# Up is kept in HBM in place of a second computation, and quantised values are rounded by 16-bit results

## The chip, the cores and the metric

The kernel runs on one core of one Trainium2 chip. The metric is the time of one execution on the device in microseconds, lower is better. The engines meant here are TensorE (PE in the profile), VectorE (DVE), ScalarE (ACT), GpSimd (POOL) and SyncE (SP), which issues transfers.

## The reference

Two decoder layers over x of 32 x 128 x 256 (batch, sequence, feature) in float32, with a context of the same shape. Each layer is a cross attention and a feed-forward part, each behind a layer norm and added to x. The change touches only the last feed-forward part, in which every tensor is quantised by its own largest absolute value:

```python
def act_qdq(x):                      # 16 bits, one scale for the whole tensor
    scale = jnp.maximum(jnp.max(jnp.abs(x)) / 32767.0, 1e-12)
    return jnp.clip(jnp.round(x / scale), -32768.0, 32767.0) * scale
def fixed_qdq_u16(x):
    return jnp.clip(jnp.round(x * 65536.0), 0.0, 65535.0) / 65536.0
x = act_qdq(layernorm(x))
up = act_qdq(x @ dequant(w_up).T)            # 4096 x 768
gate = act_qdq(x @ dequant(w_gate).T)        # 4096 x 768
sig = fixed_qdq_u16(sigmoid(gate))
gate = act_qdq(gate * sig)
o = act_qdq(gate * up)
return o @ dequant(w_down).T                 # added to x
```

Each scale needs the peak of a whole tensor of 4096 x 768 values, so nothing can be rounded before the last value of the tensor exists.

## The kernel before

The 4096 tokens lie along the free dimension, the 768 hidden features in six groups of 128 partitions (IC = 6). Work goes by "quads" of 512 tokens (NQ = 8) or by "pieces" of 256 tokens (2 x NQ = 16; 128 x 1536 elements). The whole Gate tensor stays in SBUF in float32 (`wide`, 96 KB of each partition). The quantised input stays as int16 (`xqT`) and GpSimd widens it quad by quad to float32 (`widen`, line 577, tile `xqs`, two buffers). There is no room for a second tensor like `wide`, so Up is computed twice: once for its peak alone, once for its values.

Each engine has its own hand-written program, and semaphores tie them together. In order:

- Gate (to about 849 us). `hidden` (line 1144) multiplies; ScalarE copies to `wide` (762); VectorE takes the peak (1562). `make_unit(n, count)` (1521 to 1541) turns a peak into a scale: reduce to one column, TensorE transposes it (`spread_peak(n)`, 1121) so that all partitions see all values, and eight small VectorE operations follow. Unit 1 is Gate's, 2 Up's, 3 that of Gate times sigmoid, 4 the product's, and spread_peak(n) serves unit n.
- Stage one, 16 pieces. TensorE computes Up a first time (1144, pass k = 1) and VectorE reads its peak from PSUM (1587), which frees the bank. ScalarE rounds Gate by adding the magic number 1.5 x 2^23 (777) and subtracting it (782), takes the sigmoid (788), multiplies by 65536 and adds the magic number (792). VectorE subtracts it (1592), multiplies sigmoid and Gate (1597) and takes the peak (1601). In this stage unit 2 is made after the last piece, and unit 3 right behind it. TensorE's program has spread_peak(3) behind the first quad of its next pass.
- Stage two, 8 quads. TensorE computes Up again (pass k = 2), ScalarE rounds it out of PSUM (802) and rounds the gated values (809), VectorE subtracts the magic number (1611), multiplies (1617) and takes the peak (1621).
- The tail, 32 sequences: ScalarE rounds (817), VectorE subtracts (1631), TensorE multiplies by Down (1175), VectorE adds to x (1636), SyncE stores.

The lines that set the order on TensorE between the stages:

```python
for k, freed, last_freed in ((1, up_peak, hid_kept), (2, up_round, up_peak)):
    pe.wait_ge(last_freed, NQ * IC)
    if k == 2:
        spread_peak(2)
    for t in range(2):
        hidden(t, t, wuT, k * NQ, freed)
        if k == 2 and t == 0:
            spread_peak(3)
```

Of the kernel before, what the change touches and what calls it, by code (L numbers as in the profile page):

```python
# [20 lines left out]
I16 = mybir.dt.int16  # L21
U32 = mybir.dt.uint32
# [6 lines left out]
DC = D // 128  # L29
# [18 lines left out]
LN_PARTS = (slice(0, 28), slice(28, B))  # L48
MAGIC = 1.5 * 2.0 ** 23
# [147 lines left out]
def build(nc, x, ctx_in, wq, wk, wv, wo, bq, bk, bv, bo, wfr, wfi, bf, wval, bval, woff, boff,  # L197
# [3 lines left out]
    outr = out.rearrange("b l d -> l b d")  # L201
    with ExitStack() as ctx:
# [3 lines left out]
        def sb(name, shape, dt=F32, scope=ctx):  # L206
# [20 lines left out]
        unit = sb("unit", [128, 8, 8])  # L227
        wgT = sb("wgT", [128, DC, I])
# [7 lines left out]
        wide = sb("wide", [128, IC, B * L], F32, ffn)  # L236
        xqT = sb("xqT", [128, DC, B * L], I16, ffn)
        xqs = sb("xqs", [128, 2, DC, QUAD * L], F32, ffn)
        sig_place = ExitStack()
        sig = sb("sig", [128, 2, IC, 256], F32, sig_place)  # L240
        sig_place.close()
        up_place = ExitStack()
        ups = sb("ups", [128, 2, IC, QUAD * L], F32, up_place)
        up_place.close()
# [191 lines left out]
        def _(sp):  # L436
# [7 lines left out]
            sp.dma_start(sel_f[:], c_sel).then_inc(load_sel, 16)  # L444
            sp.wait_ge(x3_done, 2 * NQ)
# [6 lines left out]
        def _(pool):  # L452
# [131 lines left out]
            with pool.Fori(0, NQ // 2) as i:  # L584
                for u in range(2):
                    widen(i * 2 + u, u, NQ)
            for t in range(2):
                widen(t, t, 2 * NQ)
            with pool.Fori(1, NQ // 2) as i:
                for u in range(2):  # L590
                    widen(i * 2 + u, u, 2 * NQ)

        @block.scalar
        def _(act):
# [180 lines left out]
            def round_gate(t, s):  # L775
                g = wide[:, :, at_piece(t)]
                nc.scalar.activation(g, g, ACT.Identity, scale=unit[:, 1, 3:4], bias=unit[:, 7, 0:1]).then_inc(g_round, 1)  # L777

            def whole_gate(t, s):
                act.wait_ge(g_round, t + 1)  # L780
                g = wide[:, :, at_piece(t)]
                nc.scalar.activation(g, g, ACT.Copy, bias=-MAGIC).then_inc(g_whole, 1)

            def sigmoid(t, s):
                act.wait_ge(g_whole, t + 1)
                if late(t, 2):
                    act.wait_ge(g2_done, t - 1)
                nc.scalar.activation(sig[:, s], wide[:, :, at_piece(t)], ACT.Sigmoid, scale=unit[:, 1, 2:3]).then_inc(sig_done, 1)

            def round_sigmoid(t, s):  # L790
                act.wait_ge(sig_done, t + 1)
                nc.scalar.activation(sig[:, s], sig[:, s], ACT.Copy, scale=65536.0, bias=MAGIC).then_inc(sig_round, 1)

            act.wait_ge(unit_step, 1 + 2 * 5)
            staggered(act, 2 * NQ, [(0, round_gate), (2, whole_gate), (5, round_sigmoid), (4, sigmoid)])

            def round_up(t, s):
                if late(t, 2):
                    act.wait_ge(o_done, t - 1)
                for oc in range(IC):  # L800
# [22 lines left out]
        def _(pe):  # L823
# [334 lines left out]
            for k, freed, last_freed in ((1, up_peak, hid_kept), (2, up_round, up_peak)):  # L1158
                pe.wait_ge(last_freed, NQ * IC)
                if k == 2:  # L1160
                    spread_peak(2)
# [498 lines left out]
```

## Time and profile before

| | |
|---|---|
| median of 3 runs | 1166.85 us (1166.5 to 1167.36) |
| the profiled execution | 1167.25 us |
| its span, first to last instruction | 1165.3 us |
| mean granted TensorE clock | 0.94 |
| busy: PE, DVE, ACT, POOL | 966.7, 739.4, 506.2, 279.5 us |
| HBM read, written | 15.22 MB, 4.19 MB |

A busy share is an average over stages that have different limits. The rows below therefore go by stage, in microseconds from the start of the span. "128x1536 f32" is a tile of 128 partitions by 1536 elements. Where two instructions of one engine follow each other closely, their busy times overlap by about 0.1 us, so the distance between their starts is the better price. One float32 matmul of the source is two records. "Idle before" is the engine's idle time ahead of an instruction, with what ended it.

### The profile page before, as it was taken

Reading aid. Unit: us, or ns where it says so; the run is one execution under the profiler, and the core shown is the slowest. Engines: PE = TensorE matmul, PEld = TensorE weight load, DVE = VectorE, ACT = ScalarE, POOL = GpSimd, SP = SyncE. Lnnn points to the kernel's source line nnn. Section 1 sums busy time; section 2 is a strip of 40 time slices with the busy share of each in tenths; the row PEclk is TensorE's granted clock in tenths of the full one; section 3 lists DMA queues with packets and bytes.
Section 4 is the critical chain, followed back from the end, with each engine's and each line's share of the span. In section 5 each row is a group of like instructions: output and inputs, shape, how many; then the busy total and the mean of one; then the engine's idle time right before and its main releaser. Section 6 shows DMA issues by size and latency. Waiting matters only on the chain.

```text
span 1165.3 us, 15427 instructions
## 1 busy us (share of the span) xinstructions
PE 966.7 (83%) x4829; PEld 599.1 (51%) x4829; DVE 739.4 (63%) x1246; ACT 506.2 (43%) x853; POOL 279.5 (24%) x251
## 2 busy tenths in 40 slices
PE   1399998899797977758888888699968975994998
PEld 1377776688465755424444444344423332441887
DVE  4377777555473566547888888744428995787333
ACT  0132221311122434346666666134369962764332
POOL 0300000132103111047877887200100010100000
PEclk9999999999898988859999999799998996997999
DMA  9500000000000000000000000000000000000111
GB/s 320 194 1 0 0 0 0 1 0 0 10 0 0 1 1 0 0 1 1 1 1 1 1 2 1 1 0 1 0 1 0 0 0 0 1 0 0 36 54 54
DMA packets 18216, 19.97 MB, mean 17 GB/s; under 512 B 1201, under 2 KB 17531, under 8 KB 18046
## 3 DMA queue, kind: packets, MB, share of 16 engines
q1 hardware_dynamic: 12950, 12.86, 3.4%
q10 hardware_dynamic: 5224, 6.57, 1.7%
q8 instruction: 24, 0.39, 0.1%
q14 instruction: 18, 0.15, 0.0%
HBM read 15.22 MB, written 4.19 MB: 17 GB/s over the span
## 4 chain that ended last, share of the span: by engine, by line
PE 38%; DVE 8%; POOL 6%; ACT 5%; issue 4%; DVEq 0%; ACTq 0%
PE pair L1144 16%; PE pair L1175 7%; POOL hat L552 4%; PE pair L1064 3%; PE pair L1078 3%; DVE peak L1587 1%; PE pair L1040 1%; PE pair L1048 1%; ACT down_b L736 1%; DVE wide L1597 1%; ACT wide L777 1%; DVE hat L1464 1%; PE pair L1090 1%; PE pair L1010 1%; PE pair L1130 1%
## 5 line engine op out<-in xcount | busy, mean ns | idle before, releaser
L1144 PE MATMUL pair<-xqs,wuT 128*128 128x512 f32 x384 | 173.9, 611 | 18.7 <-DVE peak L1587 18.0
L552 POOL TENSOR_TENSOR hat<-hat 128x1024 f32<-128x1024 f32 x62 | 145.8, 2363 | 45.6 <-DVE hat L1464 44.9
L1144 PEld LDWEIGHTS pair<-xqs,wuT 128*128 128x128 f32 x384 | 73.8, 196 | 117.4 <-issue 83.8
L1048 PE MATMUL pair<-rows,sel 32*128 32x512 bf16 x256 | 75.4, 397 | 22.9 <-ACT down_b L736 17.3
L1464 DVE SCALAR_TENSOR_TENSOR hat<-pair,down_a 128x1024 f32<-128x1024 f32 x64 | 78.2, 1222 | 24.2 <-PE pair L1040 19.7
L577 POOL CAST xqs<-xqT 128x1024 f32 (+1 forms) x24 | 25.0, 1041 | 271.0 <-PE pair L1144 192.9
L1175 PE MATMUL pair<-wdT,hid 128*128 128x256 f32 x384 | 85.5, 387 | 3.0 <-DVE hid L1631 3.0
L1464 DVE SCALAR_TENSOR_TENSOR hat<-pair,down_b 128x1024 f32<-128x1024 f32 x64 | 78.2, 1221 | 11.9 <-PE pair L1040 11.7
L736 ACT ACTIVATE down_b<-pair 128x512 f32<-128x512 f32 x128 | 69.4, 596 | 37.1 <-PE pair L1048 32.2
L1144 PE MATMUL pair<-xqs,wgT 128*128 128x512 f32 x192 | 85.2, 601 | 0.0
L736 ACT ACTIVATE down_a<-pair 128x512 f32<-128x512 f32 x128 | 69.5, 595 | 33.3 <-PE pair L1048 23.7
L1175 PEld LDWEIGHTS pair<-wdT,hid 128*128 128x128 f32 x384 | 74.6, 194 | 13.8 <-DVE hid L1631 3.2
L1064 PE MATMUL pair<-hat,vz 128*32 128x128 f32 x1056 | 69.9, 278 | 2.8 <-POOL hat L552 2.5
L1064 PEld LDWEIGHTS pair<-hat,vz 128*32 128x32 f32 x1056 | 52.9, 110 | 25.1 <-issue 24.3
L861 PE MATMUL pair<-wT,ft_sb 128*128 128x256 f32 x256 | 63.8, 392 | 0.0
L1187 DVE BATCH_NORM_STATS2 stats<-x_sb 128x6 f32<-128x256 f32 (+1 forms) x128 | 49.8, 417 | 16.5 <-DMA x_sb<-in_x_dram 16.5
L1340 DVE TENSOR_TENSOR x_sb<-pair,x_sb 128x256 f32 (+1 forms) x64 | 27.2, 424 | 51.6 <-PE pair L935 33.5
L1144 PEld LDWEIGHTS pair<-xqs,wgT 128*128 128x128 f32 x192 | 36.6, 194 | 43.6 <-issue 43.5
L817 ACT ACTIVATE hid<-wide,unit 128x768 f32 (+1 forms) x32 | 32.5, 1025 | 58.2 <-DVE hid L1631 46.1
L802 ACT ACTIVATE ups<-pair,unit 128x512 f32<-128x512 f32 x48 | 36.3, 774 | 40.1 <-PE pair L1144 40.0
L762 ACT ACTIVATE wide<-pair 128x512 f32<-128x512 f32 (+1 forms) x48 | 28.7, 597 | 56.9 <-PE pair L1144 56.9
L634 ACT ACTIVATE q_sb<-pair 128x256 f32<-128x256 f32 x32 | 12.3, 383 | 93.3 <-PE pair L865 93.3
(207 smaller groups left out, 1862.5 us busy)
## 6 DMA issues: line engine op xcount, KB each, us to landing
x_sb<-in_x_dram SPq DMA_DIRECT2D x8, 512.0 KB, 12.2
c_sb<-in_ctx_dram SPq DMA_DIRECT2D x8, 512.0 KB, 16.6
out_dram<-x_sb SPq DMA_DIRECT2D x16, 256.0 KB, 2.1
four<-in_c_four_dram ACTq DMA_DIRECT2D x1, 1280.0 KB, 12.2
deq<-in_L_ffn_w_gate_dram ACTq DMA_DIRECT2D x1, 768.0 KB, 12.7
deq<-in_L_ffn_w_up_dram ACTq DMA_DIRECT2D x1, 768.0 KB, 16.0
deq<-in_L_ffn_w_down_dram ACTq DMA_DIRECT2D x1, 768.0 KB, 16.5
big<-in_c_big_dram ACTq DMA_DIRECT2D x1, 448.0 KB
```

Source lines behind the costliest of these rows:

```text
L552: nc.gpsimd.tensor_tensor(hat[:, n % RING, :], hat[:, (n - 2) % RING, :], hat[:, n % RING, :], ALU.add).then_inc(summed, 1)
L736: nc.scalar.activation(down[n % 2][:, i, :], bank[6 + i], ACT.Relu).then_inc(down_done, 1)
L802: nc.scalar.activation(ups[:, s, oc, :], bank[2 + oc][:], ACT.Identity, scale=unit[:, 2, 3:4], bias=unit[:, 7, 0:1]).then_inc(up_round, 1)
L817: nc.scalar.activation(hid[:, 2 + s], wide[:, :, at_seq(b)], ACT.Identity, scale=unit[:, 4, 3:4], bias=unit[:, 7, 0:1]).then_inc(o_round, 1)
L861: mm(bank[2 + s][:, i * D:(i + 1) * D], ft_sb[:, s, i * DC + c, :], wT[:, i, c, :], start=False, stop=(i == 1 and c == DC - 1))
L1048: mm(bank[6 + i], sel[g:g + 32, pp, 1, :], rows[g:g + 32, q, c * 2 + a, :], start=True, stop=True).then_inc(down_mm, 1)
L1064: last = mm(bank[4 + c][32 * m:32 * m + 32, b * 128:(b + 1) * 128], vz[:, r, b, h:h + 32], hat[:, tile % RING, i * QUAD * L + b * 128:i * ...
L1078: last = mm(bank[5][:, b * D:(b + 1) * D], attT[:, c, (2 * i + b) * L:(2 * i + b + 1) * L], wout_sb[:, c, :], start=False, stop=(b == 1 an ...
L1144: last = mm(bank[2 + oc][:], w[:, c, oc * 128:(oc + 1) * 128], xqs[:, s, c, :], start=(c == 0), stop=(c == DC - 1))
L1175: last = mm(bank[s][:, 0:D], hid[:, s, ic, :], wdT[:, ic, :], start=(ic == 0), stop=(ic == IC - 1))
L1187: V.bn_stats(stats[:, at(b), :].rearrange("p o s -> p (o s)"), x_sb[:, at(b), :].rearrange("p o d -> p (o d)")).then_inc(bn_done, 1)
L1464: V.scalar_tensor_tensor(hat[:, n % RING, :], pair[n % 2][:].rearrange("p i t -> p (i t)"), 0.0, down[n % 2][:].rearrange("p i t -> p (i t ...
```

## The change

Up is computed once. TensorE works in pairs of PSUM banks (two of the six feature groups, 512 tokens; 24 pairs in all). ScalarE copies each pair to an SBUF stage of three buffers, VectorE takes the peak from there, and SyncE stores it to an HBM tensor `up_far`. After TensorE's last pair SyncE loads Up back quad by quad into three slots `ups`, which lie where the int16 input and the first stage's buffers were.

Rounding no longer uses the magic number in these two stages: an operation that multiplies by the scale writes an int16 or uint16 tile, and the conversion rounds and clamps. GpSimd does it for Gate (`whole_gate`), the sigmoid (`whole_sigmoid`) and Up (`whole_up`), ScalarE for the gated values (`whole_g2`). VectorE multiplies 16-bit tiles into float32. Both stages go by 16 halves of 256 tokens, written out instead of looped, and spread_peak(2) and (3) stand behind the last pair on TensorE. Gone are round_gate, whole_gate, round_sigmoid, round_up and round_g2 on ScalarE, the two subtractions whole_sigmoid and whole_up on VectorE, and TensorE's two passes over Up by quads. The fourth unit, the tail and all that comes before Gate are as before.

```diff
+    up_far = nc.dram_tensor("up_far", (128, NQ, IC, QUAD * L), F32, kind="Internal").ap()
+        sq = sb("sq", [128, 2, IC, 256], U16, sq_place)
+        upq = sb("upq", [128, 2, IC, 256], I16, upq_place)
+        ups = sb("ups", [128, 3, IC, QUAD * L], F32, up_place)
+        g2q = sb("g2q", [128, 4, IC, 256], I16, up_place)
-        sig = sb("sig", [128, 2, IC, 256], F32, sig_place)
-        ups = sb("ups", [128, 2, IC, QUAD * L], F32, up_place)
+        gq = sb("gq", [128, 4, IC, 256], I16, gq_place)
+        up_stage = sb("up_stage", [128, 3, 2, QUAD * L], F32, gq_place)
+        def ups_before(h):
+            return range(3 * h // 2, 3 * (h + 1) // 2)
...
@@ sync @@
+            for p in range(UPS):
+                sp.wait_ge(up_kept, p + 1)
+                sp.dma_start(up_far[:, p // 3, 2 * (p % 3):2 * (p % 3) + 2, :], up_stage[:, p % 3]).then_inc(up_stored[p % 3], 16)
+            sp.wait_ge(hid_mm, 2 * NQ * IC)
+            for t in range(NQ):
+                for j in range(3):
+                    sp.wait_ge(up_stored[j], 16 * (t + 1))
+                if t == 2:
+                    sp.wait_ge(g2_done, HALVES)
+                if t >= 3:
+                    sp.wait_ge(up_whole, 2 * (t - 2))
+                sp.dma_start(ups[:, t % 3], up_far[:, t]).then_inc(up_back[t % 3], 16)
...
@@ gpsimd @@
+            def whole_gate(h):
+                if h >= 4:
+                    pool.wait_ge(g2_done, h - 3)
+                nc.gpsimd.tensor_scalar(gq[:, h % 4], gate_half(h), unit[:, 1, 3:4], None, ALU.mult).then_inc(gate_whole, 1)
+            def whole_sigmoid(h):
+                pool.wait_ge(sig_done, h + 1)
+                if h >= 2:
+                    pool.wait_ge(g2_done, h - 1)
+                nc.gpsimd.tensor_scalar(sq[:, h % 2], gate_half(h), 65536.0, None, ALU.mult).then_inc(sig_whole, 1)
+            pool.wait_ge(unit_step, 1 + 2 * 5)
+            whole_gate(0)
+            for h in range(HALVES):
+                if h + 1 < HALVES:
+                    whole_gate(h + 1)
+                whole_sigmoid(h)
+                if h % 2 == 1 and h // 2 + 2 < NQ:
+                    widen(h // 2 + 2, h // 2 % 2, NQ)
+            def whole_up(h):
+                t = h // 2
+                if h % 2 == 0:
+                    pool.wait_ge(up_back[t % 3], 16 * (t // 3 + 1))
+                if h >= 2:
+                    pool.wait_ge(o_done, h - 1)
+                nc.gpsimd.tensor_scalar(upq[:, h % 2], ups[:, t % 3, :, h % 2 * 256:(h % 2 + 1) * 256], unit[:, 2, 3:4], None, ALU.mult).then_inc(up_whole, 1)
+            pool.wait_ge(g2_done, HALVES)
+            pool.wait_ge(unit_step, 1 + 3 * 5)
+            for h in range(HALVES):
+                whole_up(h)
...
@@ scalar @@
+            def keep_up(p):
+                act.wait_ge(hid_mm, NQ * IC + 2 * p + 2)
+                if p >= 3:
+                    act.wait_ge(up_stored[p % 3], 16 * (p // 3))
+                    act.wait_ge(up_peak, p - 2)
+                nc.scalar.activation(up_stage[:, p % 3], pair[1 + p % 3][:], ACT.Copy).then_inc(up_kept, 1)
+            def sigmoid(h):
+                act.wait_ge(gate_whole, h + 1)
+                nc.scalar.activation(gate_half(h), gq[:, h % 4], ACT.Sigmoid, scale=unit[:, 1, 2:3]).then_inc(sig_done, 1)
+            for h in range(HALVES):
+                for p in ups_before(h):
+                    keep_up(p)
+                sigmoid(h)
+            def whole_g2(h):
+                if h >= 4:
+                    act.wait_ge(o_done, h - 3)
+                nc.scalar.activation(g2q[:, h % 4], gate_half(h), ACT.Copy, scale=unit[:, 3, 3:4]).then_inc(g2_whole, 1)
+            act.wait_ge(unit_step, 1 + 4 * 5)
+            for h in range(HALVES):
+                whole_g2(h)
...
@@ tensor @@
+            def up_pair(p):
+                t, j = p // 3, p % 3
+                if j == 0:
+                    pe.wait_ge(xqs_ready, NQ + t + 1)
+                if t:
+                    pe.wait_ge(up_kept, p - 2)
+                else:
+                    pe.wait_ge(hid_kept, (NQ - 1) * IC + 2 * j + 2)
+                for oc in (2 * j, 2 * j + 1):
+                    for c in range(DC):
+                        last = mm(bank[2 + oc], wuT[:, c, oc * 128:(oc + 1) * 128], xqs[:, t % 2, c, :], start=(c == 0), stop=(c == DC - 1))
+                    last.then_inc(hid_mm, 1)
+            for p in range(UPS):
+                if p == 2:
+                    pe.wait_ge(xq_kept, B)
+                    spread_peak(1)
+                up_pair(p)
+            spread_peak(2)
+            spread_peak(3)
...
@@ vector @@
+            def peak_up(p):
+                dve.wait_ge(up_kept, p + 1)
+                V.tensor_reduce(peak[:, 2, p:p + 1], up_stage[:, p % 3], AX.XY, ALU.max, apply_absolute_value=True).then_inc(up_peak, 1)
+            def gated(h):
+                dve.wait_ge(sig_whole, h + 1)
+                V.tensor_tensor(gate_half(h), sq[:, h % 2], gq[:, h % 4], ALU.mult).then_inc(g2_done, 1)
+            for h in range(HALVES):
+                for p in ups_before(h):
+                    peak_up(p)
+                gated(h)
+                if h:
+                    peak_gated(h - 1)
+            dve.wait_ge(up_peak, UPS)
+            make_unit(2, UPS)
+            peak_gated(HALVES - 1)
+            dve.wait_ge(g2_peak, HALVES)
+            make_unit(3, HALVES)
+            def hidden_product(h):
+                dve.wait_ge(up_whole, h + 1)
+                dve.wait_ge(g2_whole, h + 1)
+                V.tensor_tensor(gate_half(h), upq[:, h % 2], g2q[:, h % 4], ALU.mult).then_inc(o_done, 1)
+            for h in range(HALVES):
+                hidden_product(h)
+                if h:
+                    peak_product(h - 1)
+            peak_product(HALVES - 1)
+            make_unit(4, HALVES)
```

## Rows read from the trace of the kernel before

**Rows 1.** Windows by stage: length, busy us (instructions) per engine, clock, DMA share, GB/s.

```profile
856.70:973.40 116.70, 81.94 (x178) 33.51 (x176) 96.51 (x96) 95.45 (x65) 8.33 (x8) 0.88 0.00 0
973.40:989.00 15.60, 15.23 (x31) 6.73 (x32) 3.04 (x16) 4.71 (x7) 1.04 (x1) 0.82 0.00 0
989.00:1073.00 84.00, 70.23 (x164) 30.78 (x162) 68.17 (x24) 53.75 (x50) 5.20 (x5) 0.95 0.00 0
...
1076.70:1165.30 88.60, 85.50 (x384) 74.56 (x384) 30.14 (x63) 30.82 (x31) 0.00 (x0) 0.97 0.14 47
```

**Rows 2.** Chain that ended last, in order of time: start, us, what.

```profile
856.67 4.78 ACT wide L777 x3
...
987.13 72.12 PE pair L1144 x168
```

**Rows 3.** Groups by line and shape from 750 us on: busy us, mean ns.

```profile
L1601 DVE TENSOR_REDUCE peak<-wide x12 | 21.0, 1749 | 0.0
...
L1592 DVE TENSOR_SCALAR sig<-sig 128x1536 f32<-128x1536 f32 x16 | 15.4, 959 | 20.2 <-ACT sig L792 20.0
...
L762 ACT ACTIVATE wide<-pair 128x512 f32<-128x512 f32 x24 | 14.3, 597 | 29.0 <-PE pair L1144 29.0
...
L1621 DVE TENSOR_REDUCE peak<-wide x4 | 13.4, 3346 | 0.0
...
L788 ACT ACTIVATE sig<-wide,unit 128x1536 f32<-128x1536 f32 x8 | 12.6, 1570 | 9.1 <-DVE wide L1597 9.1
...
L755 ACT ACTIVATE xqT<-pair 128x256 int16<-128x256 f32 x14 | 4.9, 383 | 3.2 <-PE pair L1130 2.9
...
L788 ACT ACT_TABLE_LOAD x1 | 1.3, 1283 | 0.0
```

**Rows 4.** VectorE's timeline between the stages: start, us, instruction, idle before.

```profile
968.43 1.76 DVE L1597 SCALAR_TENSOR_TENSOR wide<-sig,wide 128x1536 f32<-128x1536 f32 x1
970.09 3.42 DVE L1601 TENSOR_REDUCE peak<-wide 128x1 f32<-128x1536 f32 x2
...
975.41 0.17 DVE L1521 TENSOR_REDUCE unit<-peak 128x1 f32<-128x16 f32 x1
987.17 0.29 DVE L1523 TENSOR_REDUCE unit<-pair 128x1 f32<-128x128 f32 x1 [11.59 <-PE pair L1121]
...
1073.04 0.16 DVE L1521 TENSOR_REDUCE unit<-peak 128x1 f32<-128x8 f32 x1
```

**Rows 5.** TensorE's timeline, the two transposes and what runs before them.

```profile
849.94 5.42 PE L1144 MATMUL pair<-xqs,wuT 128*128 128x512 f32 x12 [0.69 <-ACT wide L762]
855.19 0.27 PE L1121 MATMUL pair<-big,unit 128*128 128x128 f32 x1
...
974.00 13.02 PE L1144 MATMUL pair<-xqs,wuT 128*128 128x512 f32 x24
```

**Rows 6.** GpSimd's groups over the whole span: busy us, mean ns.

```profile
L552 POOL TENSOR_TENSOR hat<-hat 128x1024 f32<-128x1024 f32 x62 | 145.8, 2363 | 45.6 <-DVE hat L1464 44.9
L577 POOL CAST xqs<-xqT 128x1024 f32 x20 | 20.8, 1041 | 239.1 <-PE pair L1144 171.0 <-ACT xqT L755 68.1
...
L468 POOL COPY cst<-c_sb 128x256 f32 x30 | 12.1, 404 | 131.5 <-PE pair L848 131.5
```

**Rows 7.** VectorE's tensor_scalar groups, and the timeline at 412 us.

```profile
L1401 DVE TENSOR_SCALAR tx<-off 128x512 f32<-128x512 f32 x4 | 7.2, 1804 | 0.0
...
L1407 DVE TENSOR_SCALAR tx<-tx 128x512 f32<-128x512 f32 x4 | 1.7, 416 | 0.0
...
412.22 2.13 POOL L518 TENSOR_TENSOR parts<-ccx,parts 128x1024 bf16<-128x1024 f32 x1 [6.26 <-ACT parts L716]
...
412.39 2.23 DVE L1401 TENSOR_SCALAR tx<-off 128x512 f32<-128x512 f32 x1
```

**Rows 8.** Transfers: a window of the loads, and the page's row of the output stores.

```profile
5.00:25.00 20.00, 3.65 (x16) 3.28 (x16) 9.84 (x28) 0.00 (x0) 0.00 (x0) 1.00 1.09 353
...
out_dram<-x_sb SPq DMA_DIRECT2D x16, 256.0 KB, 2.1
```

More of the change, by code:

```diff
@@ L772, in _ @@
             by_quad(act, keep_quad)
[L775 to L788, printed above, removed]
@@ L790, in round_sigmoid @@
-            def round_sigmoid(t, s):
-                act.wait_ge(sig_done, t + 1)
-                nc.scalar.activation(sig[:, s], sig[:, s], ACT.Copy, scale=65536.0, bias=MAGIC).then_inc(sig_round, 1)
-            act.wait_ge(unit_step, 1 + 2 * 5)
[L795 to L800, printed above, removed]
-                    act.wait_ge(hid_mm, (2 * NQ + t) * IC + oc + 1)
-                    nc.scalar.activation(ups[:, s, oc, :], bank[2 + oc][:], ACT.Identity,
-                                         scale=unit[:, 2, 3:4], bias=unit[:, 7, 0:1]).then_inc(up_round, 1)
@@ L1131, in turn_xq, with hidden @@
                 last.then_inc(xq_turned, 1)
-            def hidden(t, s, w, before, freed):
-                pe.wait_ge(xqs_ready, before + t + 1)
+            def hidden(t, s):
+                pe.wait_ge(xqs_ready, t + 1)
                 for oc in range(IC):
-                    if oc == 3 and isinstance(t, int) and t == 0 and before == NQ:
-                        pe.wait_ge(xq_kept, B)
-                        spread_peak(1)
                     if late(t, 1):
-                        pe.wait_ge(freed, (t - 1) * IC + oc + 1)
+                        pe.wait_ge(hid_kept, (t - 1) * IC + oc + 1)
                     for c in range(DC):
-                        last = mm(bank[2 + oc][:], w[:, c, oc * 128:(oc + 1) * 128], xqs[:, s, c, :], start=(c == 0), stop=(c == DC - 1))
+                        last = mm(bank[2 + oc][:], wgT[:, c, oc * 128:(oc + 1) * 128], xqs[:, s, c, :], start=(c == 0), stop=(c == DC - 1))
                     last.then_inc(hid_mm, 1)
@@ L1150, in gate_quad @@
                         turn_xq((t + 1) * QUAD + k, k % 2)
-                hidden(t, u, wgT, 0, hid_kept)
+                hidden(t, u)
             for k in range(QUAD):
@@ L1155, in _ @@
             by_quad(pe, gate_quad)
[L1158 to L1161, printed above, removed]
-                for t in range(2):
-                    hidden(t, t, wuT, k * NQ, freed)
-                    if k == 2 and t == 0:
-                        spread_peak(3)
-                with pe.Fori(1, NQ // 2) as i:
-                    for u in range(2):
-                        hidden(i * 2 + u, u, wuT, k * NQ, freed)
+            def up_pair(p):
[17 more added lines that the diff above has]
+            spread_peak(3)
             def down_product(b, s):
@@ L1581, in _ @@
             make_unit(1, NQ)
-            def peak_up(t, s):
-                for j in range(IC // 2):
-                    dve.wait_ge(hid_mm, NQ * IC + t * (IC // 2) + j + 1)
-                    V.tensor_reduce(peak[:, 2, at(t * (IC // 2) + j)], bank[2 + s * (IC // 2) + j][:], AX.X, ALU.max,
-                                    apply_absolute_value=True).then_inc(up_peak, 1)
-            def whole_sigmoid(t, s):
-                dve.wait_ge(sig_round, t + 1)
-                V.tensor_scalar(sig[:, s], sig[:, s], MAGIC, 65535.0, ALU.subtract, ALU.min).then_inc(sig_whole, 1)
```

80 lines of the change are left out of this document (29 added, 51 removed).

## The prediction

> **What bounds the kernel now.** I read the page's 40 slices first (TensorE 83% busy, no other engine over 63%), then the chain that ended last, then the windows of the last feed-forward stage by stage, because only there does the diff touch anything. The reader is to see three stages and a tail. In the sigmoid stage (856.7 to 973.4) no engine is idle long: VectorE is busy for 96.5 of 116.7 us and ScalarE for 95.5, TensorE for only 82, and its clock is at 0.88 because it stops and starts [rows 1]. In the product stage (989 to 1073) the chain is TensorE alone, 72.1 us of second Up products in 168 records [rows 2]. Between them lie 15.6 us in which VectorE works for 3 [rows 1]: the transpose that spreads the fourth peak stands behind a tile of 24 Up records that took 13.0 us [rows 5], and VectorE waited 11.6 us for the result [rows 4]. The tail, 88.6 us of Down products, is TensorE's and the change leaves it alone [rows 1].
>
> The sum below is made against the profiled execution, 1167.25 us with a span of 1165.3; the median of the runs is 1166.85, so 0.4 us less.
>
> **Stage one, start.** TensorE runs straight from Gate into Up in pairs of 8 records. A record costs 72.12/168 = 0.43 us [rows 2], a pair 3.43, a half (a pair and a half) 5.15. The second peak's transpose will stand behind two pairs, 6.9 us from 849.3, where Gate ends (849.94 less 0.69 of waiting): at 856.2 instead of 855.19 [rows 5], so 1.0 us later, and the stage starts at 857.7 instead of 856.67 [rows 2]. Then the chain of half 0 has to run: whole_gate on GpSimd (1.5, below), a table load of 1.3 and a sigmoid of 1.6 on ScalarE [rows 3], whole_sigmoid (1.5). VectorE's first product starts at about 863.1 (the table load half hidden).
>
> **Stage one, VectorE.** It loses the subtraction of the magic number (959 ns [rows 3]) and reads Up's peaks in SBUF. Starts of neighbouring 1536-element operations lie 1.66 us apart, product and reduce alike [rows 4]. From 1536 to 3072 elements a reduce grows by 3346 - 1749 = 1597 ns [rows 3], so one of 1024 is 1.66 - 0.53 = 1.13. A half is 1.5 x 1.13 + 1.66 + 1.66 = 5.0 us, against 96.5/16 = 6.0 now. The product of two 16-bit tiles into f32 has no row; I take the f32 one, and as other end the subtraction's 0.96.
>
> **Stage one, ScalarE and TensorE.** Per half ScalarE has 1.5 copies of 128x1024 from PSUM (597 ns for 512 [rows 3], and two fewer fixed parts: at most 1.2, I take 1.03) and one sigmoid of 1.6: 3.2 us where it has 95.5/16 = 6.0 now. An int16 result costs it nothing (383 ns for 256 elements [rows 3]). TensorE needs 5.15, so it and VectorE share the bound at about the same pace. ScalarE's copy of a pair waits for TensorE, for the store and for the peak of three pairs before; the sigmoid stands behind it, and with it GpSimd and VectorE. Three pairs are 10.3 us, so only TensorE's wait can last, and that is the 5.15.
>
> **Stage one, GpSimd.** This is the price that decides. Per half it gets whole_gate and whole_sigmoid (1536 elements, one f32 input, a multiplication, a 16-bit result) and half a widening of 1.04. No row shows such an operation. Lower end: its copies and casts, 404 ns for 256 and 1041 for 1024 elements [rows 6], 0.83 ns an element, so 1.47 us. Upper end: its two-input operation, 2363 ns for 1024 [rows 6], so 3.54. I take 1.5, because one input makes it most like the cast, which also changes between 16-bit and f32: 2 x 1.5 + 0.52 = 3.5 us a half, under the 5.15. The Trainium skill (GPSIMD Engine Reference, Engine selection) says that one-input operations run at roughly line rate there, which gives the same.
>
> **The shared port.** When GpSimd and VectorE overlap, one of them can stand still: VectorE's tensor_scalar of 128x512 takes 416 ns alone and 1804 where a GpSimd operation had begun just before it; the one started at 412.39 ended 0.27 us after GpSimd's 2.13 us operation from 412.22 [rows 7]. New here are GpSimd operations beside VectorE products with two SBUF inputs. Suppose that these exclude each other. GpSimd is released by the end of a product (two sq buffers; upq likewise in stage two) and then works for 3.0 or 4.0 us while VectorE has 2.8 or 3.9 of reduces, which need no second input. That fits almost, so I add only 0.25: a period of 5.25. If every product had to wait for a whole GpSimd operation it would be 6.5. The Trainium skill (SBUF — State Buffer, Who interferes with whom) says as much: a VectorE instruction with two SBUF inputs and a GpSimd one that reads SBUF block each other fully; by it my sum stands only as long as GpSimd stays short.
>
> Stage one: 863.1 + 15 x 5.25 + 1.66 = 943.5 for the last product. Then a reduce 1.66, unit 2, a reduce 1.66, unit 3; a unit without a queue in front is 1.9 to 2.0 us (from the end of the two reduces, 973.5, to 975.41 [rows 4]): 950.8 for unit 3, against 989.0. Of these 38 us, about 26 are the stage and 12 the transpose that no longer stands behind a tile.
>
> **Stage two.** whole_g2 of half 0 adds 1.6: 952.4. TensorE has nothing to do. VectorE has 16 products and 16 reduces of 1.66, 3.32 a half, and 0.08 for waits: 3.4. GpSimd's whole_up (1.5) runs under the reduce (1.66), ScalarE's whole_g2 (1.6) under both. 952.4 + 54.4 = 1006.8 for the reduce of the last peak, which stands at 1073.04 now [rows 4]. Gain 66.2: 1167.25 - 66.2 = 1101.
>
> **The transfers.** Up goes out in 24 stores of 512 KB, one per 3.43 us, and comes back in 8 loads of 1.57 MB. Loads ran at 353 GB/s and a store of 256 KB lands in 2.1 us [rows 8]; in the tail the stores kept the transfer engines 0.14 busy for 47 GB/s [rows 1], so 336 would be their full pace. A store needs 1.6 us of the engines and lands in about 3, and its buffer is wanted again after 10: hidden. A load needs 4.5 and lands in about 6.5, and a tile lasts 6.8 us; two of the three slots are filled before the stage begins, and a slot is free about four halves (13 us) before its tile is wanted: hidden. SP's queue holds only these and, behind them, the output stores. GpSimd's and ScalarE's queues hold no transfer here. Upper end: if a load ran at the pace of a single store, 256 KB in 2.1 us, it would take 12.9, and five of them after the third tile 64 us instead of the 34 that five tiles last.
>
> **The rivals.**
> *GpSimd in between.* The multiplication with conversion costs 2.3 us, a little under the middle of its two ends. With the port exclusive a half then costs 1.66 + 4.6 + 0.52 = 6.8 and in stage two 4.06: 864.8 + 102 + 8.9 + 65 = 1041, gain 32, 1135. The same time comes out if the price is 1.5 and the products mostly wait for half an operation or more. For it: rounding and clamping are more work than widening. Against: the cast's row. Chance 0.29. The Trainium skill (GPSIMD Engine Reference, Elementwise — side-by-side cycle accounting) gives bodies of three and more operations a best case of about 1.8 cycles an element; the estimate by it would be 2.3 us at the 1.2 GHz it states, and the sum this rival's.
> *GpSimd as the bound (the other side).* At 3.54 and with the port exclusive a half costs 1.66 + 7.1 + 0.52 = 9.3, and 5.3 in stage two: 864.8 + 139 + 8.9 + 85 = 1098, 24 us later than now: 1192. It decides from 3.0 us: a microsecond of price costs 30 + 16 = 46. For it: the two-input row. Against: there is one input. Chance 0.10.
> *Transfers late.* At that pace the last loads come 30 us late in all: 1131. Against: full pace was reached with several transfers at once, as here. Chance 0.04.
> *The 16-bit product is fast* (0.8 us less in stage two, TensorE bound in stage one): 1086. Chance 0.03.
> *Nothing moves:* the tail starts cold after a longer idle and instruction supply eats the rest. TensorE's Up work ends at 1059.3 now [rows 2], 17 us before the tail as well, and the tail runs at 0.97 of the clock [rows 1]. Chance 0.02.
>
> **The numbers.** The likeliest has 0.52, and alone 1091 to 1117: 4 us less if stage one holds 5.0, 1 if stage two holds 3.32, and as much again for hand-overs counted too high; 16 more if a half takes 0.5 more in both stages. The second rival, with its own spread, and the late transfers reach to 1150. 1091 to 1150 leaves out the slower case, the fast product, no move, and half of what the second rival has above 2.5 us, some 0.2 in all. Faster (by over 0.2%, which is about what measurement of this kernel can tell from no change) 0.88, same 0.02, slower 0.10.
>
> **What would show it.** GpSimd's new operations near 1.5 us; a period of 5.2 us between products in stage one, with TensorE at most 0.5 us idle between pairs; unit 3 about 7.3 us behind the last gated product; a period of 3.4 us in stage two, with VectorE over 95% busy; loads that nobody waits for; a tail of 88.6 us. GpSimd operations over 2 us, or products of over 1.76 us that end just behind a GpSimd operation, would make it wrong.

## The result, and the profile of the changed kernel

The change makes the kernel slower. Its median is 1215.29 us (4 runs, 1209.85 to 1223.42), against 1167.11 us (4 runs, 1166.5 to 1167.49) of the kernel before on the same chip: a ratio of 1.042 with a 95% interval of 1.036 to 1.048. I had forecast 1101 us, and the range ended at 1150.

The profiled execution took 1223.42 us, the longest of the four, with a span of 1221.3. First the windows of its stages, which answer to [rows 1], with the same columns.

```profile
866.20:1032.00 165.80, 85.30 (x174) 36.01 (x172) 90.76 (x57) 48.68 (x41) 158.03 (x38) 0.80 0.24 96
1036.80:1129.10 92.30, 0.00 (x0) 0.00 (x0) 57.73 (x39) 24.65 (x16) 86.01 (x16) 0.50 0.23 85
1132.60:1221.30 88.70, 85.56 (x384) 74.76 (x384) 30.15 (x63) 30.75 (x31) 0.00 (x0) 0.97 0.14 47
```

The fifth busy column is GpSimd's: 158.0 of 165.8 us in the sigmoid stage, 86.0 of 92.3 in the product stage. VectorE and TensorE are busy for about half of the first (90.8 and 85.3 us), ScalarE for 48.7 us. The tail is what it was, 88.7 us at a clock of 0.97. The page's costliest groups say the same, with what the idle engines waited for:

```profile
L1217 PE MATMUL pair<-xqs,wuT 128*128 128x512 f32 x192 | 93.4, 647 | 51.7 <-POOL xqs L606 50.6
...
L645 POOL TENSOR_SCALAR upq<-ups,unit 128x1536 int16<-128x1536 f32 x16 | 88.4, 5530 | 10.8 <-issue 9.9
L618 POOL TENSOR_SCALAR gq<-wide,unit 128x1536 int16<-128x1536 f32 x16 | 86.6, 5414 | 7.1 <-DVE unit L1595 7.1
...
L1649 DVE TENSOR_TENSOR wide<-sq,gq 128x1536 f32<-128x1536 uint16 x16 | 39.1, 2444 | 73.9 <-POOL sq L625 73.9
...
L625 POOL TENSOR_SCALAR sq<-wide 128x1536 uint16<-128x1536 f32 x16 | 65.9, 4116 | 0.0
```

GpSimd's three new operations take 5.5, 5.4 and 4.1 us where I had taken 1.5. The timeline of GpSimd and VectorE in the middle of stage one shows why two of them read longer than the third (start, duration, instruction, idle before in brackets):

```profile
866.48 8.32 POOL L618 TENSOR_SCALAR gq<-wide,unit 128x1536 int16<-128x1536 f32 x2 [7.14 <-DVE unit L1595]
...
887.65 1.03 POOL L606 CAST xqs<-xqT 128x1024 f32<-128x1024 int16 x1
888.66 5.66 POOL L618 TENSOR_SCALAR gq<-wide,unit 128x1536 int16<-128x1536 f32 x1
894.30 4.08 POOL L625 TENSOR_SCALAR sq<-wide 128x1536 uint16<-128x1536 f32 x1
898.38 5.74 POOL L618 TENSOR_SCALAR gq<-wide,unit 128x1536 int16<-128x1536 f32 x1
904.10 4.08 POOL L625 TENSOR_SCALAR sq<-wide 128x1536 uint16<-128x1536 f32 x1
908.14 1.03 POOL L606 CAST xqs<-xqT 128x1024 f32<-128x1024 int16 x1
909.15 5.66 POOL L618 TENSOR_SCALAR gq<-wide,unit 128x1536 int16<-128x1536 f32 x1
```

```profile
878.90 4.85 DVE L1649 TENSOR_TENSOR wide<-sq,gq 128x1536 f32<-128x1536 uint16 x1 [10.13 <-POOL sq L625]
...
898.41 1.76 DVE L1649 TENSOR_TENSOR wide<-sq,gq 128x1536 f32<-128x1536 uint16 x1 [5.33 <-POOL sq L625]
900.09 1.75 DVE L1654 TENSOR_REDUCE peak<-wide 128x1 f32<-128x1536 f32 x1
901.75 2.33 DVE L1644 TENSOR_REDUCE peak<-up_stage 128x1 f32<-128x1024 f32 x2
908.21 2.57 DVE L1649 TENSOR_TENSOR wide<-sq,gq 128x1536 f32<-128x1536 uint16 x1 [4.13 <-POOL sq L625]
```

The end of a sigmoid's rounding releases two instructions at once: VectorE's product and GpSimd's next gate rounding. They get in each other's way. The rounding from 898.38 spans the whole product from 898.41 and is 5.74 us long; the first two gate roundings, from 866.48, met no product and took 4.16 each, so the meeting cost 1.58, nearly the 1.66 of a product. At 878.90 it is the product that is held up, 4.85 us for 1.76 of work. In both cases GpSimd began first, by 0.03 and 0.05 us; what decides which of the two is held up stays open. GpSimd's queue is never empty, and two halves take 909.15 - 888.66 = 20.49 us, 10.25 a half. In stage two one product follows the other after 5.73 us, with 2.31 us idle:

```profile
1054.94 1.76 DVE L1672 TENSOR_TENSOR wide<-upq,g2q 128x1536 f32<-128x1536 int16 x1 [2.31 <-POOL upq L645]
1056.62 1.75 DVE L1677 TENSOR_REDUCE peak<-wide 128x1 f32<-128x1536 f32 x1
...
1060.67 1.76 DVE L1672 TENSOR_TENSOR wide<-upq,g2q 128x1536 f32<-128x1536 int16 x1 [2.31 <-POOL upq L645]
```

TensorE suffers a second time. The widening cast that feeds it stands in GpSimd's queue behind four roundings, so TensorE's timeline, to be read against [rows 5], has tiles of 24 records with 8.4 us between them:

```profile
888.74 12.06 PE L1217 MATMUL pair<-xqs,wuT 128*128 128x512 f32 x24 [8.38 <-POOL xqs L606]
909.23 12.06 PE L1217 MATMUL pair<-xqs,wuT 128*128 128x512 f32 x24 [8.43 <-POOL xqs L606]
```

The tile itself takes 12.06 us where 24 x 0.43 = 10.3 was its price at the pace of [rows 2]. Each tile starts after such an idle time, and the granted clock within one (888.74 to 900.80) is 0.87, where the stretch from 868 to 880 us, ahead of the long waits, has 1.00. It costs nothing here: TensorE still has the 8.4 us to wait.

**Balance.** I compare stages by the start of the reduction over each peak's columns ("unit<-peak"), which VectorE executes once for each peak (before: [rows 4] has those of the third and fourth). Units 1 to 4 are the scales of Gate, Up, the gated product and the hidden product.

| start of the reduction, us | before | after |
|---|---|---|
| unit 1 | 853.31 | 862.29 |
| unit 2 | 973.41 | 1032.42 |
| unit 3 | 975.41 | 1036.10 |
| last | 1073.04 | 1128.86 |
| from unit 1 to unit 2 | 120.1 | 170.1 |
| from unit 3 to last | 97.6 | 92.8 |

From unit 1 to the last one, after needs 266.6 us and before 219.7: 46.8 us more. Stage one gives 50.0 of that, the step between units 2 and 3 1.7, and stage two takes 4.9 back. The medians differ by 48.2. The profiled executions differ by 56, and 9.0 of that arise ahead of unit 1, in code that the change does not touch; the last section returns to it.

### The profile page after: what moved, and what is told of

It reads as the page before. It is cut to its first block, busy times and chain, and to the rows that moved or that the text cites. A ratio compares the mean times of both kernels' runs of the same rounds, so it can differ in the third digit from the quotient of the medians.

```text
span 1221.3 us, 14693 instructions
## 1 busy us (share of the span) xinstructions
PE 898.0 (74%) x4637; PEld 568.4 (47%) x4637; DVE 723.5 (59%) x1214; ACT 425.6 (35%) x789; POOL 511.3 (42%) x291
## 4 chain that ended last, share of the span: by engine, by line
PE 29%; POOL 17%; issue 8%; DVE 5%; ACT 3%; POOLq 0%; ACTq 0%; DVEq 0%
PE pair L1233 7%; PE pair L1192 7%; POOL sq L625 5%; POOL upq L645 4%; PE pair L1115 4%; POOL hat L581 3%; POOL gq L618 3%; PE pair L1129 3%; PE pair L1099 2%; PE pair L1091 2%; ACT down_b L795 1%; PE pair L1141 1%; DVE hat L1522 1%; PE pair L1181 1%; PE pair L1061 1%
## 5 line engine op out<-in xcount | busy, mean ns | idle before, releaser
L1217 PE MATMUL pair<-xqs,wuT 128*128 128x512 f32 x192 | 93.4, 647 | 51.7 <-POOL xqs L606 50.6
L645 POOL TENSOR_SCALAR upq<-ups,unit 128x1536 int16<-128x1536 f32 x16 | 88.4, 5530 | 10.8 <-issue 9.9
L618 POOL TENSOR_SCALAR gq<-wide,unit 128x1536 int16<-128x1536 f32 x16 | 86.6, 5414 | 7.1 <-DVE unit L1595 7.1
L1217 PEld LDWEIGHTS pair<-xqs,wuT 128*128 128x128 f32 x192 | 39.7, 212 | 104.9 <-POOL xqs L606 55.6
L1649 DVE TENSOR_TENSOR wide<-sq,gq 128x1536 f32<-128x1536 uint16 x16 | 39.1, 2444 | 73.9 <-POOL sq L625 73.9
L1115 PE MATMUL pair<-hat,vz 128*32 128x128 f32 x1056 | 76.7, 295 | 2.4 <-POOL hat L581 2.1
L497 POOL COPY cst<-c_sb 128x256 f32 (+1 forms) x32 | 15.1, 474 | 132.4 <-PE pair L899 132.4
L1115 PEld LDWEIGHTS pair<-hat,vz 128*32 128x32 f32 x1056 | 56.8, 118 | 28.2 <-issue 26.0
L625 POOL TENSOR_SCALAR sq<-wide 128x1536 uint16<-128x1536 f32 x16 | 65.9, 4116 | 0.0
L489 POOL TENSOR_TENSOR rstd<-lnt,half 128x28 f32<-128x28 f32 (+1 forms) x8 | 23.6, 2967 | 96.9 <-DVE lnt L1274 96.9
```

The costliest lines, as they stand in the source:

```text
L618: nc.gpsimd.tensor_scalar(gq[:, h % 4], gate_half(h), unit[:, 1, 3:4], None, ALU.mult).then_inc(gate_whole, 1)
L625: nc.gpsimd.tensor_scalar(sq[:, h % 2], gate_half(h), 65536.0, None, ALU.mult).then_inc(sig_whole, 1)
L645: nc.gpsimd.tensor_scalar(upq[:, h % 2], ups[:, t % 3, :, h % 2 * 256:(h % 2 + 1) * 256], unit[:, 2, 3:4], None, ALU.mult).then_inc(up_who ...
L1115: last = mm(bank[4 + c][32 * m:32 * m + 32, b * 128:(b + 1) * 128], vz[:, r, b, h:h + 32], hat[:, tile % RING, i * QUAD * L + b * 128:i * ...
L1217: last = mm(bank[2 + oc], wuT[:, c, oc * 128:(oc + 1) * 128], xqs[:, t % 2, c, :], start=(c == 0), stop=(c == DC - 1))
```

## The experiments

**A price list.** The kernel before, with GpSimd operations of one shape put into its tail on data at hand, each twice in an order, and thirty small ones beside the second Up pass. Its time of 1190.27 us in one execution (before beside it: 1167.87) holds this extra work and says nothing more; the durations are what it is for.

```diff
+            TS, TC = nc.gpsimd.tensor_scalar, nc.gpsimd.tensor_copy
+            price_list = [
+                lambda: TS(d32[:], src, 3.0, None, ALU.mult),
+                lambda: TS(d32[:], src, unit[:, 1, 3:4], None, ALU.mult),
+                lambda: TS(d16[:], src, 3.0, None, ALU.mult),
...
+                lambda: TC(d16[:], src),
...
+                lambda: TC(d32[:], src),
...
+            for k, op in enumerate(price_list * 2):
+                if k:
+                    pool.wait_ge(listed, k)
+                op().then_inc(listed, 1)
```

> The kernel before, with nothing taken out, plus GpSimd operations whose results nobody reads: in the second half of the Up stage groups of five tensor_scalar of 128x384 f32 to int16, and in the tail a price list on 128x1536 elements (tensor_scalar to f32, int16, uint16, bf16, int32; plain copies to the same; from int16). Theory A (the instruction is slow by itself: GpSimd pays for multiplication or for conversion to 16 bits): f32 to int16 takes 4.1 us in the tail too, where GpSimd is otherwise idle; if conversion is what costs, f32 to f32 takes about 1.5 and the plain copy to int16 about 4; if tensor_scalar is what costs, the reverse. Theory B (it is slow in the changed kernel because of the traffic around it, transfers and ScalarE): under 2.5 us here. Shared port: operations of 128x384 that begin with a VectorE product (3.36 us, two SBUF inputs) or subtraction (2.0) last until that one ends, up to 3 us longer; those that begin with a reduce are not longer.

GpSimd's groups in the tail of that kernel, by line and shape (`TS` is the one-factor multiplication, TENSOR_SCALAR in the profile; `TC` the plain copy, shown as CAST where the type changes):

```profile
L616 POOL TENSOR_SCALAR d<-wgT,unit 128x1536 f32<-128x1536 f32 x2 | 9.1, 4525 | 0.2
L625 POOL TENSOR_SCALAR d<-d 128x1536 f32<-128x1536 int16 x2 | 8.5, 4266 | 0.2
...
L615 POOL TENSOR_SCALAR d<-wgT 128x1536 f32<-128x1536 f32 x2 | 8.3, 4174 | 17.6 <-DVE unit L1579 17.5
L617 POOL TENSOR_SCALAR d<-wgT 128x1536 int16<-128x1536 f32 x2 | 8.3, 4173 | 0.2
...
L624 POOL CAST d<-d 128x1536 f32<-128x1536 int16 x2 | 3.3, 1672 | 0.1
L621 POOL CAST d<-wgT 128x1536 int16<-128x1536 f32 x2 | 3.3, 1664 | 0.1
L623 POOL COPY d<-wgT 128x1536 f32<-128x1536 f32 x2 | 2.9, 1468 | 0.1
```

The multiplication instruction is the price. It takes 4.17 to 4.53 us (means of two) whether it reads f32 or int16, writes f32 or int16 (or bf16, int32, uint16, all 4.26), and takes its factor from the instruction or from memory. Without it the same change of type takes 1.66, and a plain copy 1.47. The list holds no tensor_scalar with another operation, so it does not show whether the multiplication itself or every tensor_scalar is this slow. But neither the rounding nor the number of bytes is dear, and no load on memory is needed to explain the 4.08 us of the changed kernel. The same execution shows the port, which the prediction supposed that GpSimd and VectorE share, from the other side: a widening cast that takes 1.03 us elsewhere started within 0.12 us of a VectorE product of 3072 elements and took 4.14 us, ending 0.90 us behind it. Of the thirty small multiplications (128x384) most took 1.16 us and the longest 4.27, some 3 us longer, as expected.

```profile
1022.75 3.36 DVE L1655 SCALAR_TENSOR_TENSOR wide<-wide,ups 128x3072 f32<-128x3072 f32 x1 [0.86 <-ACT wide L847]
1022.87 4.14 POOL L592 CAST xqs<-xqT 128x1024 f32<-128x1024 int16 x1
```

**All three roundings on ScalarE.** The changed kernel with its stores, loads and 16-bit tiles, but `whole_gate`, `whole_sigmoid` and `whole_up` as ScalarE activations with the factor as their scale; GpSimd keeps only the widening, which so no longer stands behind roundings.

```diff
-                nc.gpsimd.tensor_scalar(gq[:, h % 4], gate_half(h), unit[:, 1, 3:4], None, ALU.mult).then_inc(gate_whole, 1)
+                nc.scalar.activation(gq[:, h % 4], gate_half(h), ACT.Copy, scale=unit[:, 1, 3:4]).then_inc(gate_whole, 1)
...
-                nc.gpsimd.tensor_scalar(sq[:, h % 2], gate_half(h), 65536.0, None, ALU.mult).then_inc(sig_whole, 1)
+                nc.scalar.activation(sq[:, h % 2], gate_half(h), ACT.Copy, scale=65536.0).then_inc(sig_whole, 1)
...
-                nc.gpsimd.tensor_scalar(upq[:, h % 2], ups[:, t % 3, :, h % 2 * 256:(h % 2 + 1) * 256], unit[:, 2, 3:4], None, ALU.mult).then_inc(up_whole, 1)
+                nc.scalar.activation(upq[:, h % 2], ups[:, t % 3, :, h % 2 * 256:(h % 2 + 1) * 256], ACT.Copy, scale=unit[:, 2, 3:4]).then_inc(up_whole, 1)
```

> The changed kernel with all three roundings of GpSimd (whole_gate, whole_sigmoid, whole_up) done by ScalarE with the same 16-bit results; the HBM round trip stays. Theory A (GpSimd's price and the port are all that is wrong): stage one takes 5.9 us a half, set by ScalarE (1.5 x 0.96 + 3 x 1.49), stage two 3.4, set by VectorE; about 1112 us. Rival (the round trip through HBM also costs): stage two stays above 5 us a half, ScalarE or VectorE waiting for loads; above 1135.

Measured: 1115.88 us (4 runs, 1112.73 to 1121.49), a ratio to the kernel before of 0.955 (0.951 to 0.959). Stage one (unit 1 to unit 2) takes 104.1 us, stage two 57.8. The bound has moved to ScalarE, busy for 90.0 of 94 us in a window of stage one, and its timeline repeats without a gap:

```profile
894.98 1.60 ACT L819 ACTIVATE gq<-wide,unit 128x1536 int16<-128x1536 f32 x1
896.44 1.59 ACT L813 ACTIVATE wide<-gq,unit 128x1536 f32<-128x1536 int16 x1
897.91 1.50 ACT L826 ACTIVATE sq<-wide 128x1536 uint16<-128x1536 f32 x1
899.28 1.04 ACT L808 ACTIVATE up_stage<-pair 128x1024 f32<-128x1024 f32 x1
900.18 1.60 ACT L819 ACTIVATE gq<-wide,unit 128x1536 int16<-128x1536 f32 x1
```

**Each stage by itself.** The same edit for `whole_up` alone, then for `whole_gate` and `whole_sigmoid` alone.

```diff
# whole_up only
-                nc.gpsimd.tensor_scalar(upq[:, h % 2], ...
...
+                nc.scalar.activation(upq[:, h % 2], ...
```

> The changed kernel with whole_up alone done by ScalarE. Theory A: stage two falls from 5.73 to 3.4 us a half, 37 us in all: about 1178 from a median of 1215. Rival (loads from HBM set stage two): under 10 us.

```diff
# whole_gate and whole_sigmoid only
-                nc.gpsimd.tensor_scalar(gq[:, h % 4], ...
-                nc.gpsimd.tensor_scalar(sq[:, h % 2], ...
...
+                nc.scalar.activation(gq[:, h % 4], ...
+                nc.scalar.activation(sq[:, h % 2], ...
```

> The changed kernel with whole_gate and whole_sigmoid done by ScalarE, whole_up left on GpSimd. Theory A: stage one falls from 10.25 to 5.9 us a half, some 67 us in all: about 1148. Stage two stays at 5.73 a half. Rival (the stores to HBM or the pair buffers hold stage one): stage one stays above 8 us a half, above 1180.

Measured: 1178.55 us (ratio 1.011, 1.008 to 1.014) and 1150.86 us (0.986, 0.983 to 0.989). The edits do not touch each other's stage:

| us | after | `whole_up` moved | gate and sigmoid moved | all three moved |
|---|---|---|---|---|
| stage one | 170.1 | 170.2 | 104.1 | 104.1 |
| stage two | 92.8 | 57.8 | 92.8 | 57.8 |
| median | 1215.29 | 1178.55 | 1150.86 | 1115.88 |

Against ScalarE's, GpSimd's multiplications cost 66 us in stage one (with what they hold back behind them in the queue) and 35 in stage two. Of the 99.4 us between the outer medians `whole_up` has 36.7 alone, and 35.0 when stage one is already mended.

**The forecast's price, given to it.** To see whether the rest of my sum stands, GpSimd's three multiplications became plain copies into the same 16-bit tiles, everything else as in the change. This kernel leaves out the multiplication by the scale, so its values are not the reference's; it serves for its time alone.

```diff
-                nc.gpsimd.tensor_scalar(gq[:, h % 4], gate_half(h), unit[:, 1, 3:4], None, ALU.mult).then_inc(gate_whole, 1)
+                nc.gpsimd.tensor_copy(gq[:, h % 4], gate_half(h)).then_inc(gate_whole, 1)
# sq and upq likewise
```

> The changed kernel with GpSimd's three tensor_scalar replaced by plain copies with the same operands and the same 16-bit results. It leaves out the multiplication by the scale, so that the rounded values are not the reference's. The price list had 1.67 us for such a copy against 4.1 to 4.3. Theory A (the forecast's schedule was right and only GpSimd's price was wrong): stage one 5.3 to 5.5 us a half, stage two 3.4 to 3.6; 1101 to 1110 us. Rival (the shared port spoils it at any price, because products and copies meet): 6.5 and 4.9 a half, above 1135.

Measured: 1103.12 us (4 runs, 1097.79 to 1104.21), ratio 0.944 (0.941 to 0.948). The timeline shows GpSimd and VectorE holding each other up here too, but at a price that fits under the reduces:

```profile
892.66 1.92 DVE L1649 TENSOR_TENSOR wide<-sq,gq 128x1536 f32<-128x1536 uint16 x1
...
895.41 1.47 POOL L625 CAST sq<-wide 128x1536 uint16<-128x1536 f32 x1 [2.43 <-ACT wide L845]
...
897.29 2.17 DVE L1649 TENSOR_TENSOR wide<-sq,gq 128x1536 f32<-128x1536 uint16 x1
...
897.80 2.99 POOL L618 CAST gq<-wide 128x1536 int16<-128x1536 f32 x1
```

A copy that meets a product takes 2.99 us for 1.46 of work. Two halves take 897.80 - 887.17 = 10.63 us, 5.32 a half (forecast 5.25), stage two 3.33 (forecast 3.4), and the reduction for the last peak starts at 1010.77 (forecast 1006.8).

**Rounding without the round trip.** The kernel before, with the 16-bit rounding on ScalarE in stage one alone; both Up passes stay and nothing goes to HBM.

```diff
-                nc.scalar.activation(g, g, ACT.Identity, scale=unit[:, 1, 3:4], bias=unit[:, 7, 0:1]).then_inc(g_round, 1)
...
-                nc.scalar.activation(g, g, ACT.Copy, bias=-MAGIC).then_inc(g_whole, 1)
...
+                nc.scalar.activation(gq[:, h % 4], gate_half(h), ACT.Copy, scale=unit[:, 1, 3:4]).then_inc(gate_whole, 1)
...
-                nc.scalar.activation(sig[:, s], sig[:, s], ACT.Copy, scale=65536.0, bias=MAGIC).then_inc(sig_round, 1)
...
+                nc.scalar.activation(sq[:, h % 2], gate_half(h), ACT.Copy, scale=65536.0).then_inc(sig_whole, 1)
...
-                V.tensor_scalar(sig[:, s], sig[:, s], MAGIC, 65535.0, ALU.subtract, ALU.min).then_inc(sig_whole, 1)
...
-                V.scalar_tensor_tensor(g, sig[:, s], 0.0, g, ALU.max, ALU.mult).then_inc(g2_done, 1)
...
+                V.tensor_tensor(gate_half(h), sq[:, h % 2], gq[:, h % 4], ALU.mult).then_inc(g2_done, 1)
```

> The kernel before, with both Up passes and no HBM, and with stage one's rounding by 16-bit results on ScalarE (three operations a half in place of four, and one less on VectorE); stage two as before. If TensorE and VectorE then set stage one: 5.2 us a half instead of 7.3, with the start some 7 us later, so 25 to 30 us less: about 1140, and the round trip through HBM is worth the rest, some 25 us, of the all-ScalarE version. Rival (the gain of that version comes from the round trip alone): under 10 us, above 1157.

Measured: 1140.14 us (4 runs, 1139.56 to 1141.58), ratio 0.977 (0.974 to 0.980), so 27.6 us less than before. Its stage one takes 94.6 us against 120.1, its stage two 96.7 against 97.6. The 24.3 us to the kernel with all roundings on ScalarE (1115.88) are what the rest of the change, the round trip with stage two's rounding, is worth on top; the two ran on different chips, where the kernel before has medians of 1167.77 and 1167.66. By the intervals it is 39.0 less in stage two, 9.5 more in stage one, where ScalarE has to copy Up out of PSUM as well, and 1.7 more between units 2 and 3: 27.8 net, of which the profiled execution with the round trip lost 5.1 again ahead of unit 1, in unchanged code.

**The late transpose alone.** The kernel before, with the transpose for the fourth peak moved ahead of the tile of Up records that it stands behind in [rows 5].

```diff
+                    spread_peak(3)
...
-                    if k == 2 and t == 0:
-                        spread_peak(3)
```

> The kernel before with one line moved: the transpose of the fourth peak stands ahead of the first tile of the second Up pass instead of behind it. Unit 3 is ready some 11 us earlier, but TensorE then starts its pass about 2.5 us later, and stage two is bound by TensorE: if so only 0 to 5 us less, 1162 to 1169. Rival (the forecast counted 12 us for it): 1155.

Measured: 1168.67 us (10 runs, 1162.47 to 1173.59), ratio 1.001 (0.999 to 1.004): nothing. The tile now runs after the transpose instead of before it, and VectorE's wait of 11.6 us for the transpose [rows 4] is replaced by one of 11.6 for the first rounded values of Up, which come out of the same tile:

```profile
974.76 0.44 PE L1121 MATMUL pair<-big,unit 128*128 128x128 f32 x1 [17.14 <-DVE unit L1520]
976.63 0.47 PE L1121 MATMUL pair<-big,unit 128*128 128x128 f32 x1 [1.43 <-DVE unit L1520]
976.90 23.68 PE L1144 MATMUL pair<-xqs,wuT 128*128 128x512 f32 x51
```

```profile
989.90 1.92 DVE L1610 TENSOR_SCALAR ups<-ups 128x3072 f32<-128x3072 f32 x1 [11.63 <-ACT ups L802]
```

Stage two of the kernel before is TensorE's 192 records from start to end, and the wait lay beside them.

**Sharing the rounding out again.** From the kernel with all roundings on ScalarE, every second `whole_sigmoid` on VectorE (0.95 us there), to relieve ScalarE in stage one.

```diff
+                V.tensor_scalar(sq[:, h % 2], gate_half(h), 65536.0, None, ALU.mult).then_inc(sig_whole_dve, 1)
...
+                if h % 2:
+                    whole_sigmoid(h)
```

> The all-ScalarE version with every second rounding of the sigmoid moved to VectorE (tensor_scalar to uint16, 0.96 us as before). ScalarE 5.0 us a half, TensorE 5.15, VectorE 5.46 instead of ScalarE 5.66: 3 us less, about 1112. Rival (VectorE's extra operation waits for the sigmoid and stalls its queue): no faster, 1116 to 1125.

Measured: 1114.01 us (4 runs, 1111.3 to 1127.08), ratio 0.957 (0.950 to 0.965). Against the 1115.88 of all three on ScalarE that cannot be told apart, and its stage one is longer, 108.3 against 104.1 us: the split gives nothing that can be measured. VectorE has become the busiest there (78.4 of 85 us from 870 on), and ScalarE, which the split was to relieve, waits 11.3 us in the same window for VectorE's reduces of Up. The expected stall of VectorE on the sigmoid is not the reason: its added rounding had no idle time ahead of it. Both beat the two kernels; the version with all roundings on ScalarE is the simpler one.

## Why the prediction was wrong

**The step that failed** is the price of GpSimd's new operations: "Lower end: its copies and casts ... so 1.47 us. Upper end: its two-input operation, 2363 ns for 1024 ... so 3.54. I take 1.5, because one input makes it most like the cast". It measured 4.08 us with the factor in the instruction and 4.16 with the factor from memory, where no product met it: outside both ends. Two things were wrong in it. The likeness: the cast has the type change in common with the new operation, the two-input operation has the arithmetic, and the list shows that the multiplication instruction, and not the type change, is what costs (4.17 against 1.66 us for the same tiles). And the upper end: I took it for granted that two inputs bound one input from above, and the profile did not say so: a multiplication by one factor costs 2.66 ns an element (4.08 / 1536), the two-input operation 2.31 (2363 / 1024). The rule of the Trainium skill (GPSIMD Engine Reference, Engine selection), that one-input operations run at roughly line rate there, holds here for copies and casts, 1.47 to 1.68 us, and not for a multiplication. The best case of about 1.8 cycles an element that the Trainium skill (GPSIMD Engine Reference, Elementwise — side-by-side cycle accounting) gives for bodies of three and more operations made an estimate of 2.3 us, which was nearer and still too low.

**The port was right in the rivals.** They had, with exclusion and for a price P, a half of 1.66 + 2P + 0.52 in stage one and, in 4.06 and 5.3, about P + 1.76 in stage two. With P = 4.08 that is 10.34 and 5.84; measured are 10.25 and 5.73. The likeliest sum had counted the port too, at 0.25 a half, which stood only as long as GpSimd was short. The Trainium skill (SBUF — State Buffer, Who interferes with whom) calls the port pair that VectorE shares with GpSimd an exclusive lock, for which a VectorE instruction with two SBUF inputs contends with a GpSimd one that reads SBUF. Most rows agree: the rounding of 5.74 for 4.16, and the cast of 1.03 that ended 0.90 us behind the product. The product of 4.85 agrees only in part, as it ended 0.74 us behind the rounding that began before it, with 1.66 of work to do.

So the outcome is the rival named GpSimd as the bound, to which I gave 0.10. At its own P of 3.54 it made 1192; each microsecond costs 46, so 4.08 would have been 1192 + 25 = 1217. That this is so near the median is in part luck, as two errors in it cancel. It starts the first product at 864.8, which suits a price of 2.3 and not three roundings one after the other: measured was 878.90, or 869.9 without the 9.0 us lost ahead of unit 1, so 5.1 later. And it counts 15 full halves of 10.34, 155.1 us, where the products from first to last took 150.2 (878.90 to 1029.09).

**The other terms**, point by point:
- Stage one's start: VectorE waited 2.80 us for the transpose behind two pairs, where it waited 2.04 before, so 0.8 later against the forecast 1.0. The first product started 16.6 us behind unit 1 where the forecast had 9.8 (863.1 less 853.31): GpSimd executes three roundings of 4.1 one after the other ahead of it. With plain copies it was 9.6.
- VectorE: a product of two 16-bit tiles is 1.76 us, as in f32; the reduce of 1024 elements takes 1.20, where 1.13 is the distance of starts. ScalarE: 1.01 us for the copy of 128x1024 (forecast 1.03), and nothing for 16-bit results (1.57).
- The version with plain copies took 0.07 a half more than my 5.25 and 0.07 less than my 3.4, and its time of 1103.12 (profiled 1104.21) stands beside the forecast of 1101. With the price right, the sum was right to 0.3%.
- The transfers are hidden: no engine waited for a load, and the loads themselves waited 56 us for GpSimd to free a slot. They landed in 6.0 us (forecast 6.5) and the stores in 2.6 (forecast 3).
- "12 the transpose that no longer stands behind a tile" was booked in the wrong place. The early transpose alone brings nothing; those microseconds are TensorE's work, and come back only because the whole second pass is removed. The total was not touched by it, as I had worked with the time at which each stage ends.
- The tail did not start cold: 88.7 us at 0.97, after 92 us in which TensorE did nothing but transposes. That rival is out.

What I did not see is that TensorE's feed would queue behind the roundings, in the queue of the engine that had become the slowest. Here it is hidden by GpSimd itself; in a version with a cheaper stage it would be the next thing to look at.

## What to carry to other kernels

Price an operation by a row with the same instruction and arithmetic, not by one with the same types or the same number of inputs; where none exists, no row of another kind is a bound, and the range must reach past it. On GpSimd keep to plain copies and casts for elementwise work (1.5 to 1.7 us for 128x1536) and let an engine that scales at little cost do the multiplication: ScalarE did the same rounding in 1.5 to 1.6 us, where its addition without a scale (782 in the kernel before) took 1.47. And before a stall is counted as a gain, ask what the other engines do during it: 11.6 us of waiting for a transpose were worth nothing by themselves, and came back as a wait of 11.6 us for something else.

## What the runs showed of the hardware that was not expected

A GpSimd multiplication of 128x1536 by one factor takes 4.08 to 4.72 us in the price list, about 2.5 times the 1.66 us of the cast between the same tiles and more for an element than the two-input operation. From start to start, too, it is 4.08 (894.30 to 898.38 in the changed kernel), so this is no matter of where a span is taken to end.

The profiled execution of the changed kernel came to unit 1 later by 9.0 us, before any changed instruction had run. The windows from 509 to 536 us and from 509 to 572, of the kernel before, the changed kernel and the one with all roundings on ScalarE, in this order (the clock is the third number from the end):

```profile
509.00:536.00 27.00, 22.16 (x130) 7.79 (x130) 17.77 (x16) 17.93 (x33) 16.63 (x13) 0.70 0.00 1
509.00:572.00 63.00, 53.30 (x415) 23.45 (x415) 47.72 (x47) 41.65 (x77) 44.74 (x32) 0.87 0.00 1
```

```profile
509.00:536.00 27.00, 24.79 (x123) 8.29 (x123) 15.72 (x13) 16.41 (x31) 16.37 (x12) 0.50 0.00 1
509.00:572.00 63.00, 59.02 (x338) 24.30 (x338) 37.87 (x35) 34.81 (x65) 37.42 (x26) 0.59 0.00 1
```

```profile
509.00:536.00 27.00, 22.76 (x106) 7.61 (x108) 15.81 (x15) 14.73 (x28) 14.03 (x12) 0.50 0.00 1
509.00:572.00 63.00, 55.60 (x366) 23.46 (x366) 42.22 (x43) 36.40 (x68) 39.91 (x27) 0.72 0.00 1
```

In these 63 us TensorE is granted 0.87 of its full clock in the first, 0.59 in the second and 0.72 in the third, and completes 415, 338 and 366 records. A clock of 0.50 is the lower of its two levels, 1.2 of 2.4 GHz. The code there is the same in all three, and the profiled executions of the other experiments show 0.88 over 490 to 600 us, as the kernel before does, against 0.69 and 0.78 in these two. Why the lower level lasted longer in two of the executions is open. It is also why medians and intervals, and not two profiled spans, carry the comparisons above.
